# Later expansion weights, two language numbers ahead, six early value rows and matrix filler at the hand-over

## The reference

```
A, Bm, emb = lora_A[lang], lora_B[lang], lang_embed[lang]        # rank 16
x = x + (x A^T) Bm^T + emb
score[s]  = tanh(x W1 + b1) . v                                  # 64 hidden units
mask[j,l] = l <= j (kind 0), l >= j (kind 1), l != j (kind 2)
p = softmax over l of (score[l] where mask[j,l])
x = x + (p x) / count of allowed l
```

## Time and profile before

| | |
|---|---|
| median of 3 runs | 118.76 us |
| the profiled execution | 118.1 us, of which the trace spans 116.3 us |
| TensorE busy | 102.6 us (88%) |
| VectorE busy | 99.3 us (85%) |
| ScalarE busy | 81.5 us (70%) |
| GpSimd busy | 28.8 us (25%) |
| HBM read, written | 17.25 MB, 8.39 MB |

### The profile page before, as it was taken

How to read it: one execution, slowest core, us unless ns; L and a number is a source line. 1 busy time by engine, 2 the same in 40 slices (tenths; PEclk the granted TensorE clock), 3 DMA queues, 4 the chain that set the end, 5 groups by cost and what they waited for, 6 DMA issues and landing times.

```text
span 116.3 us, 2490 instructions
## 1 busy us (share of the span) xinstructions
PE 102.6 (88%) x606; PEld 81.6 (70%) x606; DVE 99.3 (85%) x244; ACT 81.5 (70%) x168; POOL 28.8 (25%) x84
## 2 busy tenths in 40 slices
PE   7939999999999999993999989999899989989930
PEld 2718788996989778881587666777687767767820
DVE  5724999999778899999839999968999999999980
ACT  1966755687699999984172877878878889885300
POOL 6736852235766682100030210000000000000000
PEclk9999999999999999999589999999999999999995
DMA  3999999999999999920002406413445253345463
GB/s 89 256 312 379 385 377 383 377 376 379 377 375 377 369 386 374 322 71 0 6 0 93 180 21 252 177 51 144 183 180 182 88 206 144 130 168 186 180 229 135
DMA packets 16104, 25.87 MB, mean 223 GB/s; under 512 B 1256, under 2 KB 10024, under 8 KB 16090
## 3 DMA queue, kind: packets, MB, share of 16 engines
q1 hardware_dynamic: 15912, 25.44, 61.6%
q10 hardware_dynamic: 178, 0.27, 0.8%
HBM read 17.25 MB, written 8.39 MB: 220 GB/s over the span
## 4 chain that ended last, share of the span: by engine, by line
DVE 42%; PE 32%; issue 11%; DMA 6%; ACT 5%; SPq 1%; DVEq 0%
DVE o L819 18%; PE psum L418 13%; DVE yl L773 10%; PE psum L493 8%; DMA xT<-in_x_t 6%; DVE x L722 5%; PE psum L427 4%; DVE tT L711 3%; PE psum L436 3%; ACT yh L616 2%; PE psum L468 2%; PE psum L472 2%; DVE rz L847 2%; ACT tT L582 2%; ACT tanh L589 1%
## 5 line engine op out<-in xcount | busy, mean ns | idle before, releaser
L493 PE MATMUL psum<-yh,q 128*128 128x258 f32 x128 | 34.9, 304 | 3.8 <-DVE o L819 3.3
L418 PE MATMUL psum<-xT,wsel 128*128 128x256 f32 x128 | 30.6, 382 | 1.9 <-DMA xT<-in_x_t 1.9
L493 PE MATMUL psum<-yl,q 128*128 128x258 f32 x128 | 32.1, 282 | 0.0
L493 PEld LDWEIGHTS psum<-yh,q 128*128 128x128 f32 x128 | 24.3, 190 | 8.7 <-issue 8.3
L624 ACT ACTIVATE q<-psum 128x512 fp32r<-128x512 f32 x32 | 19.1, 597 | 14.7 <-PE psum L472 14.6
L773 DVE SCALAR_TENSOR_TENSOR yl<-x,g_col,yh 128x258 fp32r<-128x258 f32 x64 | 29.3, 483 | 0.1
L616 ACT ACTIVATE yh<-x,g_col 128x258 fp32r<-128x258 f32 x64 | 28.9, 501 | 0.2
L418 PEld LDWEIGHTS psum<-xT,wsel 128*128 128x128 f32 x128 | 24.0, 190 | 5.6 <-DMA xT<-in_x_t 2.4
L819 DVE SCALAR_TENSOR_TENSOR o<-psum,rz,x 128x256 f32<-128x256 f32 x64 | 27.1, 481 | 0.5 <-DVE rz L830 0.3
L493 PEld LDWEIGHTS psum<-yl,q 128*128 128x128 f32 x128 | 24.4, 191 | 0.0
L351 POOL COPY wsel<-wall 128x256 f32 x32 | 13.0, 416 | 15.6 <-PE psum L418 12.6
(11 more groups left out here) (96 smaller groups left out, 72.6 us busy)
## 6 DMA issues: line engine op xcount, KB each, us to landing
xT<-in_x_t SPq DMA_DIRECT2D x16, 512.0 KB, 8.1
x<-in_x_n SPq DMA_DIRECT2D x16, 512.0 KB, 9.5
out<-o SPq DMA_DIRECT2D x31, 256.0 KB, 2.0
out<-o SPq DMA_DIRECT2D x2, 128.0 KB, 2.1
o<-in_b_nat ACTq DMA_DIRECT2D x1, 200.0 KB
w_in<-in_w_pack SPq DMA_DIRECT2D x1, 196.5 KB, 2.5
n_arg<-n_part SPq DMA_DIRECT2D x8, 4.0 KB
m_arg<-m_part SPq DMA_DIRECT2D x8, 4.0 KB
```

The source lines that it names most:

```text
L418: last = nc.tensor.matmul(proj_ps[b // 2 % 2][:, b % 2 * S:(b % 2 + 1) * S], wsel[:, b % V, c, :], xT[:, b % RING, c, :], start=(c == 0), ...
L493: last = nc.tensor.matmul(pool_ps[SLOTS[b]][:, j, 0:DZ], q[:, b % V, s, j * P:(j + 1) * P], part_y[:, b % VY, s, :], start=(s + k == 0), s ...
```

## The change

It has five parts. (1) `b_in` is loaded by ScalarE's queue after the wait for `w_in` and after `kindr_i`, no longer before them. (2) GpSimd reads two language numbers ahead of the first `select`, not four, and the seven small memsets ahead of them move behind `select(3)`; ScalarE's wait for them moves to p = 5. (3) `ON_POOL` becomes 7, 9, 11: three items, earlier. (4) Only six value rows are made early (`NE` = 6); rows 6 and 7 move to the second stage, `high_y` to b = 0 and 1, `low_y` to b = 2 and 3; in iteration 5 `low_t` goes ahead of `fraction(0, 1)`. (5) At the hand-over TensorE waits for `g_ready` (set by `column(0)`) and runs two 512-column products of constants into bank 6, between the register reads and `expand`.

```diff
-    ON_POOL = (11, 13, 15, 17)
+    NE = 6
+    ON_POOL = (7, 9, 11)
...
-            nc.gpsimd.memset(x1[:, 0:B // 2, :, D:DZ], 1.0)
-            nc.gpsimd.memset(x1[:, B // 2:B, :, D:DZ], 1.0).then_inc(tails_ready, 1)
-            for t, value in ((0, 1.0), (1, 0.0), (2, 2.0)):
-                nc.gpsimd.memset(forbidden[:, t:t + 1], value)
-            nc.gpsimd.memset(rounds[:, 0:1], ROUND)
-            nc.gpsimd.memset(rounds[:, 1:2], -ROUND).then_inc(tails_ready, 1)
...
-            first = [language(b) for b in range(V)]
+            first = [language(b) for b in range(2)]
             pool.wait_ge(wall_ready, 3)
             for b in range(B):
-                select(b, first[b] if b < V else language(b))
+                select(b, first[b] if b < 2 else language(b))
                 if b == 3:
+                    nc.gpsimd.memset(x1[:, 0:B // 2, :, D:DZ], 1.0)
...
-            def keep_warm(n):
+            def keep_warm(n, of=7):
                 for _ in range(n):
-                    nc.tensor.matmul(bank[7][:, :], nc.const_aps.tensor(1.0, (P, P), bf16),
+                    nc.tensor.matmul(bank[of][:, :], nc.const_aps.tensor(1.0, (P, P), bf16),
...
             kinds = [kind_of(0), kind_of(1)]
+            pe.wait_ge(g_ready, 1)
+            keep_warm(2, 6)
             expand(B - 2, langs[0])
...
-            act.dma_start(b_in, b_nat).then_inc(b_loaded, 16)
             act.wait_ge(consts, 1)
...
             act.wait_ge(w_loaded, 16)
+            act.dma_start(b_in, b_nat).then_inc(b_loaded, 16)
...
-                if EARLY_STEP <= p < EARLY_STEP + FIRST[1]:
+                if EARLY_STEP <= p < EARLY_STEP + NE:
                     high_y(p - EARLY_STEP)
...
             for b in range(B):
                 if b + 2 < B:
                     powers(b + 2)
+                if b < FIRST[1] - NE:
+                    high_y(NE + b)
...
                 if p == 5:
                     fraction(0, 0)
+                low_t(p)
+                if p == 5:
                     fraction(0, 1)
-                low_t(p)
...
-                if EARLY_STEP < p <= EARLY_STEP + FIRST[1]:
+                if EARLY_STEP < p <= EARLY_STEP + NE:
...
+                if b in (2, 3):
+                    for s in range(NS):
+                        low_y(NE + b - 2, s)
```

More of the change, by code:

```diff
@@ L381, in _ @@
             pool.wait_ge(ids_loaded, 16)
-            first = [language(b) for b in range(V)]
+            first = [language(b) for b in range(2)]
             pool.wait_ge(wall_ready, 3)
             for b in range(B):
-                select(b, first[b] if b < V else language(b))
+                select(b, first[b] if b < 2 else language(b))
                 if b == 3:
+                    nc.gpsimd.memset(x1[:, 0:B // 2, :, D:DZ], 1.0)
+                    nc.gpsimd.memset(x1[:, B // 2:B, :, D:DZ], 1.0).then_inc(tails_ready, 1)
+                    for t, value in ((0, 1.0), (1, 0.0), (2, 2.0)):
+                        nc.gpsimd.memset(forbidden[:, t:t + 1], value)
+                    nc.gpsimd.memset(rounds[:, 0:1], ROUND)
+                    nc.gpsimd.memset(rounds[:, 1:2], -ROUND).then_inc(tails_ready, 1)
                     nc.gpsimd.affine_select(out=identb[:], in_=ones[:], compare_op=ALU.is_equal, fill=0.0, base=0,
@@ L575, in _ @@
             act.wait_ge(tT_ones, 1)
-            act.wait_ge(tails_ready, 3)
             def high_t(p):
@@ L635, in _ @@
                 if p == 5:
+                    act.wait_ge(tails_ready, 3)
                     whole(0)
@@ L651, in _ @@
                     grow(0)
-                if p == NP - 1:
-                    for k in range(p - EARLY_STEP + 1, FIRST[1]):
-                        high_y(k)
             powers(0)
@@ L809, in _ @@
             add_lora(NP - 1)
-            for k in range(NP - EARLY_STEP - 1, FIRST[1]):
-                for s in range(NS):
-                    low_y(k, s)
             def divide(b, k):
```

## The result

The changed kernel takes 124.64 us (median of 4 runs, 123.43 to 125.81) against 118.5 us: a ratio of 1.0506, 95% interval 1.0385 to 1.0627. The forecast of 120.4 us and its range to 122.2 were wrong; rival (b), late expansion weights, is what happened. The profiled execution took 125.81 us, span 124.0; it is 1% above the median and the one slow run of the four, left out of the ratio, but its mean granted clock, 0.965, is like the 0.962 and 0.964 of two of the others.

A forecast was written before the change was run, and what follows sets the result against it. VectorE, closely followed by TensorE, was taken to bound the second stage. Start +0.5, hand-over +0.2 and second stage +1.8 on the profiled 118.1 us gave 120.6; 120.4 us was forecast, between that and a 120.1 case, range 117.2 to 122.2.

The forecast's parts named there:

- rival (b): Start, ScalarE's wait at L568: expansion weights land late, +3.7 us (123.8) with the 8.1 us of `xT`, halfway 122.5; chance 0.17.
- the size in part 1: Start: the later `b_in` load takes 4.9 us and lands at 8.5, so step 1 ends 0.5 us later.
- The issue time: Start: `b_in` issued at 3.6 us, behind the wait for `w_in`, 1.5 us later than before.
- the way from landing to `expand`: Start: cast to end of `wallB`, then `low_t(0)` and handing on, 4.5 us from `b_in` landing to first `expand`.
- Part 2: Start: first `select` at about 6.7 us, then the first `xT` limits; gain 0 to 0.6 us for steps 0 and 1.
- Part 3: First stage: ScalarE's slow pairs go, VectorE takes adds; `low_t(14)` at 50.7 instead of 50.99, -0.26 us.
- Part 4: Two rows return to the second stage on full VectorE, +1.8 us; earlier `low_t(15)` doesn't move the last `expand`.
- Rival (c): Start gains 0.6 us, hand-over +0.2 and -1.45, VectorE's slack hides the two second-stage rows: 116.4 us; chance 0.15.
- Part 5: Hand-over: filler adds 0.45 us before `expand`; keeping the clock would give 1.45 us, but it was forecast to fall.
- Rival (a): Hand-over: TensorE's clock stays at 2.4 GHz, -1.45 us, 119.1 us; chance 0.25.
- Its price on the path: Hand-over: two 512-column filler products between the register reads and `expand` cost +0.45 us.

The follow-up runs named there:

- two_ahead: `p1_only` with SyncE holding everything behind the second `xT` until `strip` is made; two runs, 118.28 and 121.05 us, no ratio.
- hold_sync: `p1_only` with SyncE issuing only the first `xT`, then waiting until `strip` is made; 117.49 us, ratio 0.9975 against the kernel before.
- tail_held: `p1_only` with SyncE issuing its first four loads, then none until `b_in` has landed; 123.58 us, ratio 1.0465 against the kernel before.
- p1_only: The kernel before with part 1 alone, `b_in` issued behind the wait for `w_in`; 124.69 us, ratio 1.0561.
- part2_only: The kernel before with part 2 alone, two language numbers ahead and the seven memsets moved; 117.70 us, ratio 0.9997.
- p4_only: The kernel before with part 4's six early value rows alone; 119.72 us, ratio 1.0171.
- reads_early: The kernel before with all four hand-over register reads moved ahead of the last step's `expand`; 117.33 us, ratio 0.9958.
- part3_only: The kernel before with part 3, `ON_POOL` = 7, 9, 11, and `low_t(5)` ahead of `fraction(0, 1)`; 117.35 us, ratio 0.9978.
- undo_p1: The changed kernel with `b_in` issued at its old place, parts 2 to 5 kept; 118.49 us, ratio 1.0068 against the kernel before.
- p5_only: The kernel before with the two filler products alone; 117.60 us, ratio 0.9976.
- spread: The kernel before with the four hand-over register reads made one each in steps 11 to 14; 117.44 us, ratio 0.9960.
- spread_fill: `spread` with five 512-column filler products between the last score and the last `expand`; 116.98 us, ratio 0.9918 against the kernel before.

## Why the prediction was wrong

**The step that failed is the size in part 1.** The load was priced at 4.9 us from its own 5.56 us and from rising GB/s, with 5.56 as the upper end of the own range; it took 9.18. The issue time (3.6, measured 3.38) and the way from landing to `expand` (4.5, measured 4.61) were right. The price was taken as a function of the rate around it, while the loads standing ahead of it set it. At its old place, 2.11 us, it went out beside the second `xT` (2.06), so two of these loads at most stood ahead of it, not four, and its 5.56 us are close to the 5.71 of `two_ahead`. The trace held this: the order of the issues on both queues. `hold_sync`, `two_ahead` and `tail_held` show it. The page "DMA: Bandwidth & Descriptors" of the Trainium skill (section "Issuing engines are not separate DMA queues") was read as an argument against a long wait. That transfers of both issuers share 16 engines and interleave is true here as far as the later ones go, +1.7 us; it didn't let `b_in` pass the earlier ones, and the measurement decides.

**A term was missing.** With a wait that long TensorE is idle 4.32 us, and the clock goes to 1.2 GHz behind it: +2.91 us, where the rival counted the delay alone. `p1_only` lost it too behind an idle time of 5.5 us (+1.6), `tail_held` behind one of 3.85; in `two_ahead`, with 1.79, the clock was kept at the start. Rival (b), by its far end of 8.1 us, gave 123.8, near the 124.64, with a chance of 0.17. Its mechanism is right, its nearness is luck: it had 3.7 us at the start where the profiles have 7.65, and +0.2 us at the hand-over where they have -1.1.

**Part 2** was expected to give 0 to 0.6 us and gave nothing. In the profiles of the change and of `part2_only` the first `select` waited for `wall`, which TensorE delivered late. The four products that `wall` needs, in the kernel before and in the change:

```profile
5.01 1.10 PE L509 MATMUL psum<-fold,a_in 128*128 128x256 f32 x4 [0.15 <-DVE fold L687]
```

```profile
5.16 2.02 PE L510 MATMUL psum<-fold,a_in 128*128 128x256 f32 x4
```

They took 2.02 us in all five kept profiles of kernels with part 2, and in three of the eleven without it, `p4_only`, `reads_early` and `part3_only`. So part 2 is not the only thing that can slow them; whether it has a hand in it, or five times was chance, stays open. What part 2 gives where they take 1.10 was not seen in any profile.

**Part 3** had its mechanism and sign (-0.26 forecast, -0.40 in its own profile and -0.60 in the change's, ratio not clear of 1).

**Part 4** was right in mechanism and size: +1.8 forecast, +1.76 twice and +1.73; no gain at the hand-over, because the reads set the last `expand`. Rival (c), VectorE hiding the rows, is refuted.

**Part 5** went better than forecast, and the reason given for it was wrong. Rival (a), that the clock stays, had a chance of 0.25, because 2.0 us of idle time stay ahead of the filler. They do stay, and yet the clock was kept in the profiles of the change, of `undo_p1` and of `p5_only`. Single profiles can't show that the filler did this: `part2_only` and `part3_only` have no filler, 2.03 us of idle time, and kept the clock too, while the kernel before, `p4_only` and `hold_sync` lost it at 2.02 and 2.03. That fits what the Trainium skill says in "TensorE: Matmul & The Clock Gate", section "What's actually happening", of a watch that runs free of the kernel.

The mean granted clock of every execution can show it. In the profile of before TensorE had 1.2 GHz from 55.5 to 58.9 us; half of these 3.4 us is missing from a span of 116, so the mean is 0.985 or less. Of the 31 executions of the kernel before beside `p5_only`, 18 are at or under that; of the ten of `p5_only`, which has the filler and nothing else, none is (lowest 0.993). Of the 19 beside `undo_p1` 11 are, of its ten none (lowest 0.987). `spread` has three in ten, `spread_fill` none. Some of the 29 may owe it to the end of the execution, where the clock falls too; but the kernels with filler have that end as well. So the filler kept the clock. How it does so with the same idle time ahead of it is not shown.

Its price on the path was forecast as 0.45 us. From `low_t(14)` to the last `expand` it is 0.39 us, but most of this comes back behind it. From the end of the idle time to item 0's sum it is 3.67 us with the filler (`p5_only` and the change) and 3.57 without it where the clock stayed (`part2_only`, `part3_only`), so the filler cost 0.1 us; where the clock fell it is 4.80 (before) and 4.78 (`hold_sync`), so the clock is worth 1.2 us there, not 1.45. Over whole executions it is worth less: those of before at or under 0.985 have a median of 117.96 us, the others 117.50 (31 executions), and 117.98 against 117.34 (19). In the profiles of `part2_only` and `part3_only`, which kept it, the first `expand` came at 12.98 and 13.14, in those of before and `hold_sync`, which lost it, at 12.44 and 12.11: the executions without filler that kept the clock had started later. With 0.46 us saved in 18 of 31 executions and 0.1 us paid in all, `p5_only` should gain 0.17 us; it gained 0.19. `spread_fill` fell short of its forecast for the same reason.

**What stays open**: the sum of the parts alone (0, -0.2, +1.7, -0.2%) is 1.3%, and `undo_p1` has 0.7% (0.4 to 1.0); the intervals allow for it, and no run explains more. Nor was it tried how much the transfers behind `b_in` matter at its old place, where its cast began between 7.1 and 9.0 us in these profiles.

## What to carry to other kernels

A small load that many steps wait for must be costed by what has been issued before it on every queue, not by its own time at another place: one load of 512 KB more ahead of it was 2 us here. Before work is moved off an engine "because it ends late", look at what its consumer is doing, register reads included, and at whether the place where the work lands is the one where that engine is full. Filler is best placed where the idle time begins, as in `spread_fill`; behind what causes the idle time it was still worth having here, 0.1 us for a clock that was kept in all 20 executions. And one profile doesn't tell whether a clock is kept: count executions.

## What the hardware showed

- Loads issued by ScalarE wait for those issued earlier by SyncE: 3.6, 5.7, 7.9 and 9.6 us to landing with one, two, four, and four (and a crowd behind) loads of `x` or `xT` ahead. Up to 4.7 us of it pass before the first packet moves.
- A read of one number into a TensorE register is 0.3 us for the load alone and 0.65 us from one to the next. Four in a row left the engine idle 2.0 us.
- The same 2.0 us of idle time cost TensorE its clock in some executions (1.2 us up to the first sum) and not in others. Two 512-column products of constants behind that idle time kept it in 20 executions of 20, where the kernel before, by its mean granted clock, kept it for certain in 21 of 50.
